# A state-space layer on one core: shifted copies staged in halves in the first group, row loads ahead of weight loads, and another order at the last group's end

## What is computed

```python
proj = hidden_states @ in_proj_w.T
gate, xBC, dt = jnp.split(proj, [INTER, INTER + CONV_DIM], axis=-1)
xBC = silu(conv(xBC))                       # depthwise, 4 taps
x, Bm, Cm = jnp.split(xBC, [INTER, INTER + NG * SS], axis=-1)
...
cs = jnp.cumsum(dA, axis=-1)                # per head
seg = cs[..., :, None] - cs[..., None, :]
Lmat = jnp.where(tri, jnp.exp(seg), 0.0)
scores = jnp.einsum('bclhn,bcshn->bchls', Cc, Bc) * Lmat
Ydiag = jnp.einsum('bchls,bcshp->bclhp', scores, xdt)
...
yg = y * silu(gate)
out = (yg * rsqrt(mean(yg ** 2 per group) + EPS)) * norm_w
return out @ out_proj_w.T
```

## Time and profile before

| | |
|---|---|
| median of 3 runs | 2177.77 us (2177.53 to 2183.19) |
| profiled execution | 2182.37 us, its span 2180.5 us |
| PE (matmul) busy | 2082.0 us, 95% of the span |
| PE weight loads | 1567.6 us, 72% |
| DVE | 1587.5 us, 73% |
| ACT | 1189.0 us, 55% |
| POOL | 819.0 us, 38% |
| DMA | 285.39 MB, mean 131 GB/s |
| row loads | 252 issues of 384 KB, median 4.0 us to landing |
| stage | 63 times 1024 KB (12.1 us) and 512 KB (14.2 us) |
| input weights | 144 issues of 256 KB, 6.5 us |

### The profile page before, as it was taken

One profiled execution on the slowest core, in us unless ns is written; L12 is line 12 of the kernel. 1 busy time (PEld: TensorE's weight loads), 2 busy tenths in 40 slices (PEclk: granted clock), 3 DMA queues, 4 the chain that ended last, 5 costly groups with the idle time before them and its releaser, 6 DMA issues. The chain is left out here.

```text
span 2180.5 us, 38225 instructions
## 1 busy us (share of the span) xinstructions
PE 2082.0 (95%) x11176; PEld 1567.6 (72%) x11176; DVE 1587.5 (73%) x3212; ACT 1189.0 (55%) x2858; POOL 819.0 (38%) x692
## 2 busy tenths in 40 slices
PE   7899899998989999999999999999999999989998
PEld 4555555446767887887877787787787787767877
DVE  5675757657877699599589779859958967967345
ACT  5554545314765576377368457647737744854330
POOL 4352524211444255145335425424523532553220
PEclk9899999999999999999999999999999999999999
DMA  6000000005999778788877968878787896812101
GB/s 248 20 17 1 1 1 1 15 0 148 213 208 201 170 186 189 146 204 196 161 170 199 171 169 197 174 153 194 189 161 177 200 168 164 187 49 88 48 10 39
DMA packets 243108, 285.39 MB, mean 131 GB/s; under 512 B 9424, under 2 KB 210896, under 8 KB 242256
## 3 DMA queue, kind: packets, MB, share of 16 engines
q1 hardware_dynamic: 242896, 282.86, 55.2%
HBM read 280.20 MB, written 103.02 MB: 176 GB/s over the span
## 5 line engine op out<-in xcount | busy, mean ns | idle before, releaser
L2026 PE MATMUL ab_ps<-xh_keep,wh 128*128 128x512 f32 x1148 | 456.7, 398 | 2.7 <-DVE yt L1767 2.3
L2028 PE MATMUL ab_ps<-xh_keep,wl 128*128 128x512 f32 x1148 | 448.1, 390 | 0.0
L2027 PE MATMUL ab_ps<-xl_keep,wh 128*128 128x512 f32 x1148 | 446.8, 389 | 0.0
L1720 DVE SCALAR_TENSOR_TENSOR xs<-ab_ps,par,xs 128x510 f32<-128x510 f32 (+2 forms) x384 | 284.8, 742 | 45.2 <-ACT xs L1387 31.8
L1606 POOL TENSOR_TENSOR wl<-raw_weights,wh 128x512 fp32r<-128x512 f32 x141 | 183.2, 1299 | 313.3 <-ACT wh L1366 311.6
L1748 DVE TENSOR_TENSOR decayed<-ab_ps,b_scores 128x384 f32<-128x384 f32 x512 | 266.5, 549 | 30.1 <-ACT ab_ps L1416 21.0
L1415 ACT ACTIVATE ab_ps<-rows,ncs 128x256 f32<-128x256 f32 x512 | 239.8, 468 | 63.6 <-DMA rows<-skewed_rows 31.6
L2026 PEld LDWEIGHTS ab_ps<-xh_keep,wh 128*128 128x128 f32 x1148 | 215.8, 188 | 49.3 <-issue 4.8
L2028 PEld LDWEIGHTS ab_ps<-xh_keep,wl 128*128 128x128 f32 x1148 | 215.5, 188 | 46.7
L2027 PEld LDWEIGHTS ab_ps<-xl_keep,wh 128*128 128x128 f32 x1148 | 216.0, 188 | 42.4
L1627 POOL TENSOR_TENSOR ssq<-ssq,sq 128x512 f32<-128x512 f32 x112 | 144.5, 1290 | 228.9 <-ACT sq L1424 228.9
(11 more groups left out here) (280 smaller groups left out, 4074.9 us busy)
## 6 DMA issues: line engine op xcount, KB each, us to landing
rows<-skewed_rows SPq DMA_DIRECT2D x252, 384.0 KB, 4.0
skewed_rows<-sum_rows SPq DMA_DIRECT2D x63, 1024.0 KB, 12.1
raw_weights<-win_dram SPq DMA_DIRECT2D x144, 256.0 KB, 6.5
skewed_rows<-sum_rows SPq DMA_DIRECT2D x63, 512.0 KB, 14.2
qkv_or_out_weights<-wout_dram SPq DMA_DIRECT2D x8, 2048.0 KB, 9.0
raw_weights<-wgu_dram SPq DMA_DIRECT2D x11, 512.0 KB, 3.5
w<-w_dram SPq DMA_DIRECT2D x1, 3584.0 KB, 17.7
draw<-wd_dram SPq DMA_DIRECT2D x1, 2816.0 KB, 10.4
```

The lines of the kernel that those rows point to most:

```text
L1720: ins = nc.vector.scalar_tensor_tensor(y[:, :, back:], z[:, :, 0:SEQ - back], param(g, sub, TAPS - 1 - back), y[:, :, back:], ALU.mult, AL ...
L2026: nc.tensor.matmul(out, w_h, x_h, start=(k == 0), stop=False)
L2027: nc.tensor.matmul(out, w_h, x_l, start=False, stop=False)
L2028: last = nc.tensor.matmul(out, w_l, x_h, start=False, stop=(k == KT - 1))
```

## The change

Three edits to the lists.

1. In the first group, units 2 to 8 are staged by `stage_pair`, four DMAs for two of the four b. The pair (3, 0) of a unit goes out where the whole stage stood, at the end of a step, and the pair (1, 2) in the next step, behind the row load of b = 0. The row load of b = 0 waits for the first pair (64 on the semaphore), those of b = 1, 2 and 3 for both (128); `staged_at` gives the counts. Unit 1 and all units from 9 on are staged whole, as before.
2. In each step of every group the row load of b = 0 stands ahead of the first weight load, and that of b = 1 ahead of the second.
3. At the end of the last group: ACT rounds the output weights of step 2 inside unit 7; the second square of unit 6 moves behind the high part of y of step 2, its addition on POOL behind the gate of unit 7; the work of steps 4 and 5 moves between and ahead of the last squares; and DVE makes the low part of y of step 1 in unit 7, behind the silus, and not at the end of unit 6.

```diff
--- before.py
+++ after.py
@@ -1295,6 +1295,22 @@
                                  bass.AP(tensor=src, offset=s0 + shift, ap=[[1, P], [ROW, 2 * BATCH], [1, cols]]))\
                         .then_inc(staged[n % 8], 16)
 
+            def stage_pair(n, pair):
+
+                src, dst = ssm["rows"].tensor, ssm["skewed"].tensor
+                for b in pair:
+                    s0, d0 = (2 * n * BATCH + b) * ROW, n % STAGED * P * WIDE + b * ROW
+                    for at, shift, cols in ((0, 0, SEQ), (SEQ, P, P)):
+                        sp.dma_start(bass.AP(tensor=dst, offset=d0 + at, ap=[[WIDE + 1, P], [BATCH * ROW, 2], [1, cols]]),
+                                     bass.AP(tensor=src, offset=s0 + shift, ap=[[1, P], [BATCH * ROW, 2], [1, cols]]))\
+                            .then_inc(staged[n % 8], 16)
+
+            def staged_at(n, b):
+
+                if 2 <= n <= UNITS:
+                    return 128 if b else 64
+                return 32 * ((n - 1) // 8) + (32 if n % 8 == 1 else 128)
+
             def load_rows(n, b):
 
                 if n >= NG * UNITS:
@@ -1302,7 +1318,7 @@
                 g, j = (n - 1) // UNITS, (n - 1) % UNITS
                 ph = Phase("loop", g, g) if g < LOOPS else Phase("epi", 0, g)
                 sp.wait_ge(*bk.filled(ph, f"E{j}_{b}_1"))
-                sp.wait_ge(staged[n % 8], 32 * ((n - 1) // 8 + 1))
+                sp.wait_ge(staged[n % 8], staged_at(n, b))
                 sp.dma_start(rows[:, b], bass.AP(tensor=ssm["skewed"].tensor, offset=n % STAGED * P * WIDE + b * ROW,
                                                  ap=[[WIDE, P], [BATCH * ROW, 2], [1, ROW]])).then_inc(rows_loaded[b], 16)
 
@@ -1328,14 +1344,19 @@
                     more = g < LOOPS or 8 + 2 * j < SUBS
                     if g and not j:
                         load_out(g)
+                    load_rows(n + 1, 0)
                     if more:
                         load_in(g, 8 + 2 * j)
-                    load_rows(n + 1, 0)
+                    if not g and j:
+                        stage_pair(j + 1, (1, 2))
+                    load_rows(n + 1, 1)
                     if more:
                         load_in(g, 9 + 2 * j)
-                    for b in range(1, BATCH):
-                        load_rows(n + 1, b)
-                    if not g:
+                    load_rows(n + 1, 2)
+                    load_rows(n + 1, 3)
+                    if not g and j < LAST:
+                        stage_pair(j + 2, (3, 0))
+                    elif not g:
                         stage(j + 2)
                     elif j % 2 == 0:
                         stage(g * UNITS + 5 + j // 2)
@@ -1429,22 +1450,30 @@
                 nc.scalar.activation(yh[:, h, :], yg[:, j, h * HALF:(h + 1) * HALF], ACT.Copy,
                                      scale=param(g, 2 + j, TAPS + 2)).then_inc(*y_hi.inc())
 
-            def end_hi(ph, g, n):
-
-                j, h = ENDS[n]
+            def end_weights_hi(ph, g, n):
+
                 if n >= 2:
                     act.wait_ge(*end_used(ph, n - 2))
                 else:
                     act.wait_ge(o_loaded.sem, g * 16 + 16)
-                nc.scalar.activation(oh[:, n % 2, :], oraw[:, j, :], ACT.Copy).then_inc(o_hi.sem, 1)
+                nc.scalar.activation(oh[:, n % 2, :], oraw[:, ENDS[n][0], :], ACT.Copy).then_inc(o_hi.sem, 1)
+
+            def end_y_hi(ph, g, n):
+
+                j, h = ENDS[n]
                 if n < 2:
                     act.wait_ge(*gated.made(ph, f"{j}_{h}"))
                 nc.scalar.activation(yh[:, n % 2, :], yg[:, j, h * HALF:(h + 1) * HALF], ACT.Copy,
                                      scale=param(g, 2 + j, TAPS + 2)).then_inc(*y_hi.inc())
 
+            def end_hi(ph, g, n):
+
+                end_weights_hi(ph, g, n)
+                end_y_hi(ph, g, n)
+
             def end(ph, g):
 
-                for n in range(4, 2 * UNITS):
+                for n in range(6, 2 * UNITS):
                     end_hi(ph, g, n)
                 for t in range(NT // 2, NT):
                     act.wait_ge(*bk.filled(ph, f"xT{t}"))
@@ -1504,9 +1533,11 @@
                         tanh(ph, h[0])
                     if more:
                         weights_hi(g, 7 + 2 * j)
+                    if last and final:
+                        end_weights_hi(ph, g, 2)
                     next(e[3])
                     next(e[3])
-                    if j:
+                    if j and not (last and final):
                         square(ph, j - 1, 1)
                     if h and final:
                         tap(ph, gn, h[2])
@@ -1588,9 +1619,12 @@
                 project(ph, i)
             ph = Phase("epi", 0, LOOPS)
             steps(ph, LOOPS, True)
-            end_hi(ph, LOOPS, 2)
+            end_y_hi(ph, LOOPS, 2)
+            square(ph, LAST - 1, 1)
             end_hi(ph, LOOPS, 3)
             square(ph, LAST, 0)
+            end_hi(ph, LOOPS, 4)
+            end_hi(ph, LOOPS, 5)
             square(ph, LAST, 1)
             end(ph, LOOPS)
 
@@ -1638,7 +1672,7 @@
                         gate(ph, j - 1, 1)
                     if more:
                         weights_lo(g, 7 + 2 * j)
-                    if j:
+                    if j and not (last and j == LAST):
                         add_square(ph, j - 1, 1)
                     if j == LAST - 1:
                         out_weights_lo(g, 0)
@@ -1677,11 +1711,14 @@
 
             end_weights(2)
             gate(ph, LAST, 0)
+            add_square(ph, LAST - 1, 1)
             end_weights(3)
             gate(ph, LAST, 1)
+            end_weights(4)
             add_square(ph, LAST, 0)
+            end_weights(5)
             add_square(ph, LAST, 1)
-            for n in range(4, 2 * UNITS):
+            for n in range(6, 2 * UNITS):
                 end_weights(n)
             for n, w in ((0, 0), (0, 1), (1, 0)):
                 cols = slice(w * KT * P, (w + 1) * KT * P)
@@ -1788,6 +1825,7 @@
                     if final and last:
                         silu(ph, conv_halves(j)[2])
                         silu(ph, conv_halves(j)[3])
+                        end_lo(ph, g, 1)
                     if j:
                         skip(ph, g, j - 1, 1)
                         times_dt(ph, g, j, 0)
@@ -1824,9 +1862,9 @@
                         skip(ph, g, j, 1)
                         taps(ph, gn, h[3])
                         silu(ph, h[2])
-                    if last and LAST - 2 <= j < LAST:
-                        end_lo(ph, g, j - (LAST - 2))
-                    elif LAST - 2 <= j < LAST:
+                    if last and j == LAST - 2:
+                        end_lo(ph, g, 0)
+                    elif not last and LAST - 2 <= j < LAST:
                         out_lo(ph, g, 0, LAST - 1 - j)
 
             def crossing(ph, g):
```

## The result

The changed kernel takes 2209.90 us (median, 2206.47 to 2212.88) against 2178.11 us before (2177.53 to 2183.19): a ratio of 1.0142, 95% interval 1.0128 to 1.0156, so 1.4% slower. The side was as forecast, the size was not: +31.8 us where I had worked out +9.7, and outside the range of 2175 to 2194. The profiled execution took 2206.47 us, its span 2204.6 us, 24.1 us more than the span before.

A forecast was written before the change was run, and what follows sets the result against it. The first group was taken as bound by a closed loop of SP and DMA engines, the last group's end by PE. +15.1 (staging) + 0 (load order) - 5.4 (end) = +9.7 us on the median 2177.77: 2187.5, range 2175 to 2194.

The forecast's parts named there:

- The period: First group's units: 14.5 us of data plus two gaps of 2.8 us, 20.1 us a unit instead of 17.3.
- the price of a half: First group, each staged pair of 768 KB: 4.55 us of data, then 2.8 us of gap before dependent rows start.
- My upper bound for a half: First group: a staged pair takes 5.0 us instead of 4.55, the unit lasts 21.0 us, the loss is 20.5.
- The lower bounds: First group: each staged pair adds a gap of at least 2.4 us, the unit lasts 19.7 us, the loss is 12.7.
- the rule of the Trainium skill: First group: 2.0 us fixed cost per DMA as added gap, unit 19.3 us, kernel some 4.5 us under forecast.
- The cover of slice 23: First group's end: weight slice makes ACT 3.1 us late, hidden by its 3.64 us wait for PE; 0, at most 3.
- The order of loads in the other groups: Row loads ahead of weight loads delay a weight load by 4 us, hidden by the ring of three: 0.
- The end: End of last group: PE waits less for POOL's low parts, the mean of squares starts 5.4 us earlier.
- worse: Staged pair at 5.0 us, slice 23 uncovered by 1, end gaining 4: 2195; chance 0.14 together with the end failing.
- Less costly halves: First group: gap under about 2.2 us or pair at 4.2, loss 6 to 11, kernel 2178 to 2183; chance 0.24.
- faster: First group: each staged pair keeps stage's quick initial speed, 2.8 us, unit 16.6 us, kernel 2166.5; chance 0.10.
- The end doesn't deliver: Last group: step 2 or 4 waits for DVE or ACT, gain 1 not 5.4, 2192; chance 0.14 together with worse.

## Why the prediction was wrong

**The bound, and what goes into the loop: right.** Row load b = 1 of unit 2 went out 10.2 us behind b = 0 (9.05 worked out). That b = 0 itself went out at 564.19, where I had 564.4, is luck: that of unit 1 stood at 548.81 and not 551.67, and the step between them took 15.4 us and not 12.75, mostly because pair (3, 0) could only go out at 553.94, behind row loads that wait for exps of unit 0. Two gaps a period are there, ACT waits ahead of b = 1 for 7.24 us, later groups keep their pace, and no compute engine is in the loop.

**The period: 20.1 us worked out, 21.6 measured; this is the step that failed.** The part from b = 1 to b = 0 came out (11.0 us), the part from b = 0 to b = 1 was 10.6 us where 9.05 stood. The term at fault is the price of a half, 4.55 us of data and 2.8 us of gap. It took a half to move at the rate of a whole, and pair (1, 2) with its gap took 1.55 us longer. The run with eight small DMAs and one wait shows 0.9 to 1.7 us more a period for their size or number, and the exchanged pairs show that the slow part is (1, 2). The gaps were 2.7 and 3.6 us where 2.8 stood twice, so in the part that came out a longer gap was made up by quicker data. Over six periods the idle share is 3.5 and 3.2 us in the two parts; where the gap begins in a share that thins out is a choice, so the 1.5 us can't be divided more finely between gap and data. Five periods turned it into 8 us, and the first part of unit 2 was 0.9 us late: unit 7's exps start at 686.45 where 677.6 was worked out. My upper bound for a half, 5.0 us, reached a loss of 20.5 us in the units; 21.9 was measured. The lower bounds (2.4 us for the gap) didn't matter.

The sentence on the rule of the Trainium skill (about 2.0 us of fixed cost for each DMA, in DMA: Bandwidth & Descriptors, Anatomy of one DMA) named the right direction. That section fits its figure on DMAs that GpSimd issues, which the prediction left out; here SP issues them. The second wait cost 3.4 us a period by the run without it, more than that figure, and here the measurement decides. A gap in this loop has the thinning out of the last packets in it too: the share is 0.46 and 0.14 in the two us from 616 to 618, before it is 0.

**The cover of slice 23: +4.1 us where 0 stood, and 3 at most.** I had it arrive 3.1 us late and set that against the 3.64 us for which ACT waits for PE at 691.52. It was 5.70 us late: part 1 of unit 8 went out 18.0 us behind unit 7's exps instead of 16.5, the error of the period once more, and the slice landed more than 1 us later behind it than worked out. There is a cover, but it isn't that row's. ACT rounds slice 23 23.3 us behind unit 7's exps and not 17.5, and the first high part of y at 713.33 is only 2.2 us late: shorter waits in between took 3.6 us. The wait for PE behind it took nothing in, but grew to 5.46 us at 719.50, as PE's projection was late as well, and 4.1 us came through. A lateness of 2.85 us, with the pairs exchanged, cost 0.5, so with the 3.1 us of the sum the 0 would nearly have held. What failed is first the size of the lateness, and then the cover for what lies beyond 3 us. That PE's projection came late through the tanhs and squares behind the weights in ACT's list, which feed DVE and POOL, is an argument from the lists; no run tests it.

**The order of loads in the other groups: right**, 0. In the first group it is 0 alone, but not together with the halves, where it comes to some 10 to 12 us with slice 23's part in it. The sum had only slice 23 there, at 0.

**The end: nearly right.** 5.4 us worked out, 4.4 in the traces, 5.0 by the medians of the run with the end alone. The mean of squares came 1 us later than worked out: POOL's low part 3 was ready 0.4 us late, because the square ahead of it took 1.73 and not 1.3 us, and steps 3 to 5 took 8.9 us (1968.21 to 1977.13) where I had 8.35. The last group shows 3.7 and not 4.4: from its first exps to its last the changed kernel takes 0.7 us more. The ten traces differ by 3 us in that stretch, whichever end they have.

**The base: a loss read from an unusual execution.** I made the sum on a profiled execution that was 4.3 us over the median of its kernel, and laid it on the median. In that profile units 1 to 7 take 103.2 us; in the traces of the two kernels that keep the whole stages, 16.5 and 16.7 us a unit, they take 93.9. Against those the changed kernel's 125.1 us are a loss of 31.2 us and not 21.9. The medians differ by 31.8 us and the two profiled spans by 24.1: the profile before lies 4.3 us over its median, the one after 3.4 us under its own.

**The rivals.** The case "worse" came nearest (2195): it had both mis-sized terms in it, a half at my upper bound (20.5 us of loss, 21.9 measured) and slice 23 at 1 us (4.1 measured). "Less costly halves" and "faster" are out: a half starts at 311 GB/s, but goes on at 83 to 130, so the quick start doesn't hold for a whole half. "The end doesn't deliver" is out by the run with the end alone.

## What to carry to other kernels

Before a transfer that gates the next in a closed loop is cut in two, look for something else that stands in the DMA queue while each part lands: here nothing did, the extra dependent wait cost 3.4 us a unit, and queueing one more whole unit ahead took the gap away. When an instruction in an in-order list is held by a new wait, check each instruction behind it against the lateness that the new loop gives, not against the old one; an order that costs nothing alone can cost with such a wait in it. And before a sum is laid on a median, see by how much the term's base varies from one execution to another; a range built from one trace is too narrow when the term is multiplied by a loop.

## What the runs showed of the hardware

- The same 1536 KB between two places in device memory, in pieces of 1 KB and 512 bytes: cut into eight DMAs instead of two, and waited for once, a period of the loop takes 18.2 us against 16.5 to 17.3. SP takes 7 to 8 us to issue the eight and 1.3 to 2.5 us to issue the two. Which of number, size, order and issue time does it stays open.
- Of two equal halves of such a copy one is steadily slower: with (3, 0) in the middle and (1, 2) at the end the parts take 9.6 and 12.3 us, the other way round 10.6 and 11.0. In the period shown above the DMA share falls to 0.65 and 0.79 in the middle of the slower one. In the exchanged run, where (1, 2) goes last, it stays at 0.94 to 1.02 from 623 to 629 us but for one us at 0.74, while the rate falls to 81 GB/s at the end, so the fall of the share isn't the whole of it. The cause stays open.
- With a copy always queued, the DMA engines moved 254 GB/s at a share of 1.07, in the loop that ran at 213 to 223 GB/s and 0.85 to 0.91 in three traces with a drained queue.
